# Self-attention of a four-layer transformer block: a lead of 14 query units in place of 22, work by query halves, first operands spread by token halves

## Chip, core and metric

The kernel runs on one core of one Trainium2 chip. The time is the device time of one execution, in microseconds, of which the median of several runs counts. A profile is of one execution.

## What is computed

Two batch entries of 1024 tokens and 256 features pass through four layers. The change is in the self-attention of the third (cut):

```python
x_norm = modulate(_ln(x), shift_a, scale_a)
qkv = x_norm @ W_qkv + b_qkv
q, k, v = jnp.split(qkv, 3, axis=-1)      # 16 heads of 16 features
attn_w = jax.nn.softmax(jnp.einsum('bhqd,bhkd->bhqk', q, k) * scale, axis=-1)
attn_out = jnp.einsum('bhqk,bhkd->bqhd', attn_w, v)
x = x + gate_a[:, None] * (attn_out @ W_proj + b_proj)
```

All is in float32. The layers before (cross-attention, a routed mixture of experts) and behind (cross-attention to a context, two MLPs, windowed attention, attention to the 16 best keys) are not touched.

## The kernel before

There is no planner. Each engine has one program written out by hand, and semaphores tie them. The loop `for b in range(B)` runs over the two batch entries. Within it the self-attention stage works on pairs of heads, eight of them. P is 128 (partitions), T = 8 token tiles, BLK = 512 tokens, TB = 4 tiles in a block, NP = 8 pairs, UNITS = 128.

**Operands.** Queries and keys are kept as a rounded high part and a low part (`dense`: q_hi, q_lo, k_hi, k_lo), so that a score is a product of three terms of 16 rows each, 48 rows. `linear` on TensorE makes the product of one block of tokens, ScalarE (`high_part`, L1434) writes the high part with its bias, VectorE (`low_part`, L2246) the low one. For a pair, `spread(p)` on GpSimd (L2543) copies rows of `dense` to the rows of `qx` and `kx` that the scores read: 12 DMAs of 64 KB a pair, rows 0 to 47 for one head and 64 to 111 for the other. Of `qx` and `kx` there are four places, so pairs 0 to 3 are spread before the loop and pair p + 3 in it. `c_fill` fills four constant rows behind each head's 48.

The `dense` tiles hold eight heads. The other eight are made by `full_step` (L973) on TensorE, from the same block of hT, and copied by ScalarE into `full`, which lies over hT. Once all four pairs have been spread out of `dense`, ScalarE copies `full` over it (L1662), and GpSimd forms the low parts (L2574).

**Units.** A unit is one head and one tile of 128 queries (or keys). `query_scores` (L984) writes 128 queries x 1024 keys with two matmuls; VectorE reduces them to the maximum (`query_maximum`, L2251). After 16 units, a pair, `maxima` (L2256, L2257) splits the maxima in a high and a low part, TensorE transposes them (`turn_maxima`, L991), ScalarE copies them (`maximum_rows`, L1632), and GpSimd sends them by four DMAs (L2553) into rows 48, 49, 112 and 113 of `qx`. So `key_scores` (L999), which writes 128 keys x 512 queries, twice a unit, already subtracts the maximum. ScalarE takes the exponential (`probabilities`, L1640), `weigh_values` (L1011) multiplies with the values, eight matmuls a unit, and `finish` (L1021, L2262) transposes and divides.

**Order.** One loop `for n in range(-LEAD, UNITS)` is written in each engine's program. At step n the key side works on unit n and the query side on unit m = n + LEAD. For the first LEAD steps only query scores are made, for the last LEAD steps only key scores. The query scores take turns in two double banks of PSUM (`take`), the key scores in three banks (`take_key`), so TensorE runs two units ahead of VectorE at most. Steps are in order on each engine: TensorE's wait for the rows of maxima (`mrow_ld`) at the first unit of a pair holds the query scores behind it too.

In the lead TensorE also has four of the eight steps of `full_step`, three small matmuls that spread the gates (L1059), and `keep_busy` (L591): matmuls of a constant tile whose product nobody reads. Ahead of the lead stand `values(1)` (L938), four steps of `full_step` and more `keep_busy`.

The SyncE program loads weights of the layers behind (5.25 MB, L430) while the stage before ends, from 222.8 to 230.3 us.

## Time and profile before

| | us |
|---|---|
| median of 3 runs | 1604.02 (1602.52 to 1604.21) |
| the profiled execution | 1601.8 |
| its span | 1600.0 |
| TensorE matmul busy | 1490.6 (93%) |
| VectorE busy | 1050.8 (66%) |
| ScalarE busy | 769.6 (48%) |
| GpSimd busy | 377.6 (24%) |
| mean granted clock of TensorE | 0.987 |
| self-attention, first query scores to last maximum | 248.3 to 423.4, and again 768 us later |

Busy is the time in which an engine worked; a matmul's end is modelled, so that a busy TensorE can still be one that waits inside. A row in order of time gives the start, the duration, the engine, the line of the kernel, the operation, what it writes and reads, the shapes and how many instructions are merged in it; in brackets how long the engine was idle before and what ended that. Times are from the start of the span. An output of one float32 matmul can be two records.

### The profile page before, as it was taken

How to read it: one execution, taken by the hardware profiler on the slowest of the kernel's cores; microseconds unless marked ns; L12 is line 12 of the kernel's file. 1: busy time of each engine (PE TensorE's matmuls, PEld its weight loads, DVE VectorE, ACT ScalarE, POOL GpSimd, SP SyncE). 2: the span in 40 equal slices, each digit the busy share in tenths (PEclk: the TensorE clock that was granted, in tenths of full speed). 3: DMA queues.
4: the chain of work that ended last, by engine and by line, in shares of the span. 5: the costliest groups of instructions: out<-in, count | busy, mean ns of one | idle time of the engine just before them, and what ended most of it. 6: DMA issues, size and time to landing. Idle time of an engine off the chain costs nothing.

```text
span 1600.0 us, 26614 instructions
## 1 busy us (share of the span) xinstructions
PE 1490.6 (93%) x10593; PEld 937.2 (59%) x10593; DVE 1050.8 (66%) x2960; ACT 769.6 (48%) x1232; POOL 377.6 (24%) x419
## 2 busy tenths in 40 slices
PE   5899999999999999987999999999999999998898
PEld 3457765444355857656765767544445475765676
DVE  2574456999537446899457535599972745579963
ACT  1335421788844533325543543168885363333454
POOL 4420006342125110114133000634210701001330
PEclk9999999999999999999999999999999999999999
DMA  9500037121020000000130001812102000000000
GB/s 339 164 0 1 0 112 106 21 42 22 2 79 1 1 0 3 2 1 1 46 125 1 1 1 61 157 22 36 27 2 79 1 1 1 2 2 1 1 1 27
DMA packets 37663, 59.81 MB, mean 37 GB/s; under 512 B 7347, under 2 KB 27091, under 8 KB 36643
## 3 DMA queue, kind: packets, MB, share of 16 engines
q1 hardware_dynamic: 25239, 34.71, 6.6%
q0 software_dynamic: 9520, 16.04, 6.2%
q10 hardware_dynamic: 2780, 7.36, 1.3%
q8 instruction: 83, 1.36, 0.4%
q14 instruction: 41, 0.34, 0.1%
HBM read 42.22 MB, written 2.10 MB: 28 GB/s over the span
## 4 chain that ended last, share of the span: by engine, by line
PE 66%; DVE 21%; issue 6%; ACT 3%; DMA 1%; POOL 1%; ACTq 0%; DVEq 0%; POOLq 0%
PE ps L999 10%; PE ps L1011 9%; PE ps L463 5%; PE ps L1321 4%; PE ps L984 3%; PE ps L591 3%; PE ps L1112 3%; DVE taken L2384 3%; DVE rs L2062 3%; PE ps L1346 2%; PE ps L1103 2%; DVE taken L2396 2%; DVE mxw L2054 2%; PE ps L1173 2%; PE ps L599 2%
## 5 line engine op out<-in xcount | busy, mean ns | idle before, releaser
L2251 DVE TENSOR_REDUCE mm<-ps 128x1 f32<-128x1024 f32 x256 | 310.5, 1223 | 35.1 <-PE ps L984 31.7
L1640 ACT ACTIVATE pt<-ps 128x512 f32<-128x512 f32 x512 | 276.8, 600 | 61.0 <-PE ps L999 43.6
L2502 POOL TENSOR_TENSOR rstd<-ve,minus_half 128x4 f32<-128x4 f32 x32 | 34.9, 1091 | 695.3 <-DVE ve L1926 695.3
L999 PE MATMUL ps<-qx,kx 64*128 64x512 f32 x512 | 188.5, 445 | 1.0 <-ACT pt L1640 1.0
L984 PE MATMUL ps<-kx,qx 48*128 48x512 f32 x512 | 186.7, 444 | 0.2
L1011 PE MATMUL ps<-pt,v 128*32 128x256 f32 x2048 | 158.7, 390 | 0.0
L999 PEld LDWEIGHTS ps<-qx,kx 64*128 64x128 f32 x512 | 79.0, 184 | 95.9 <-ACT pt L1640 85.9
L591 PE MATMUL ps<-filler 128*128 128x512 f32 x382 | 119.8, 440 | 0.0
L2139 DVE TENSOR_TENSOR rlo<-ring,rhi 128x512 fp32r<-128x512 f32 x48 | 33.2, 691 | 91.9 <-ACT ring L1590 91.9
L1011 PEld LDWEIGHTS ps<-pt,v 128*32 128x32 f32 x2048 | 42.9, 108 | 85.5 <-ACT pt L1640 61.3
L984 PEld LDWEIGHTS ps<-kx,qx 48*128 48x128 f32 x512 | 75.4, 185 | 24.4 <-issue 19.3
L591 PEld LDWEIGHTS ps<-filler 128*128 128x128 f32 x382 | 69.5, 194 | 32.9 <-issue 22.7
L2553 POOL DMA_DIRECT2D qx<-mxT x64 | 33.3, 527 | 209.4 <-ACT mxT L1632 189.3
L2015 DVE TENSOR_TENSOR x<-x,ps 128x512 f32<-128x512 f32 x64 | 41.7, 683 | 50.9 <-PE ps L615 27.5
L1590 ACT ACTIVATE rhi<-ps,mod 128x512 fp32r<-128x512 f32 x48 | 33.1, 690 | 69.1 <-PE ps L783 69.0
L2339 DVE TENSOR_REDUCE mxw<-ps 128x8 f32<-128x1024 f32 x32 | 38.8, 1224 | 37.5 <-PE ps L1173 37.5
L2625 POOL TENSOR_TENSOR prob<-prob,m 128x1024 f32<-128x1024 f32 x16 | 31.0, 1936 | 126.2 <-DVE taken L2384 126.2
L2054 DVE TENSOR_REDUCE mxw<-ps 128x16 f32<-128x1024 f32 x32 | 37.7, 1220 | 34.6 <-PE ps L649 34.6
L1732 ACT ACTIVATE wprobT<-ps 128x1024 f32<-128x1024 f32 x32 | 32.7, 1023 | 56.6 <-PE ps L1199 56.3
L1933 DVE TENSOR_SCALAR xhat<-x,mv,rstd 128x256 f32<-128x256 f32 x128 | 46.3, 425 | 18.9 <-POOL rstd L2502 18.7
L2062 DVE RECIPROCAL rs<-ps 128x512 f32<-128x512 f32 x16 | 53.7, 3355 | 7.3 <-PE ps L686 7.3
L1434 ACT ACTIVATE hT<-ps,mod 128x512 f32<-128x512 f32 x48 | 34.7, 776 | 38.4 <-PE ps L599 38.4
(374 smaller groups left out, 3319.7 us busy)
## 6 DMA issues: line engine op xcount, KB each, us to landing
wm<-in_L_xcond_W_mlp_dram SPq DMA_DIRECT2D x4, 1024.0 KB, 8.6
qx<-q_hi POOLq DMA_DIRECT2D x64, 64.0 KB, 2.5
kx<-k_hi POOLq DMA_DIRECT2D x64, 64.0 KB, 2.5
w3a<-in_L_xcond_w_m_dram SPq DMA_DIRECT2D x2, 2048.0 KB, 7.6
w<-in_L_xcond_e_w_dram SPq DMA_DIRECT2D x6, 512.0 KB, 7.9
w<-in_L_xcond_e_w_dram SPq DMA_DIRECT2D x2, 1536.0 KB, 12.8
s_ada<-in_L_xcond_w_ada_dram ACTq DMA_DIRECT2D x1, 2304.0 KB, 23.3
qx<-q_lo POOLq DMA_DIRECT2D x32, 64.0 KB, 2.4
```

Of the source, the lines that this page charges most:

```text
L463: ins = pe.matmul(ps[:, bank, :], w[:, c, m * P:(m + 1) * P], src[:, c, :], start=c == 0, stop=c == KC - 1)
L591: pe.matmul(ps[:, bank, :], filler[:, 0:P], filler[:, :], start=True, stop=True)
L984: ins = pe.matmul(ps[:, bank + half, :], qx[r, p % 4, t * P:(t + 1) * P], kx[r, p % 4, half * 512:(half + 1) * 512], start=True, stop=True)
L999: pe.matmul(ps[:, bank, :], kx[r, p % 4, kc * P:(kc + 1) * P], qx[r, p % 4, half * 512:(half + 1) * 512], start=True, stop=True).then_inc( ...
L1011: ins = pe.matmul(ps[o:o + 32, 7, q:q + BLK // 2], v2[:, kc, VS * (2 * p + e):VS * (2 * p + e) + 32], pt[:, (2 * kc + e) % 8, half * BLK + ...
L1112: ins = pe.matmul(ps[:, 4 + 2 * k + j, :], w2s[:, wp, m, j * P:(j + 1) * P], gelus[sp][:, m % 4, :], start=m == 0 and (wp, sp) == (0, 0), ...
L1321: ins = pe.matmul(ps[:, 4 + i, :], w3ap[wp][:, c, (NC_HID * i + m) * P:(NC_HID * i + m + 1) * P], src[:, c, :], start=(wp, part, c) == (0, ...
L1640: act.activation(pt[:, u % 8, half * 512:(half + 1) * 512], ps[:, bank, :], ACT.Exp, scale=QK_SCALE).then_inc(st_read, 1)
L2054: ins = dve.tensor_reduce(mxw[:, t, :].rearrange("p (r n) -> p r n", r=4)[:, :, 0:4], ps[:, bank:bank + 4, o:o + D].rearrange("p r (h s) - ...
L2062: link(dve.reciprocal(rs2[:, u % 2, :], ps[:, bank + 1, :]))
L2251: return dve.tensor_reduce(mm[:, p % 2, e, t:t + 1], place(), X, ALU.max).then_inc(ring_read, 1)
L2384: ins = dve.match_replace(taken_by_head(t)[:, h, :], m8[:, t % 2, h, 0:8], scores_by_head(t)[:, h, :], LOWEST)
```

## The change

- LEAD is 14. The first eight units of pair 0 are cut another way: each has both heads, one tile of the first 512 queries, and one half of the keys. After eight units the maxima of the first 512 queries are complete. Their two parts are combined by one more small step.
- Maxima are split, turned, copied and sent after each eight units, the first 512 queries and then the others. A turn has half the rows, and a half is sent by two DMAs of two rows in place of four of one row for the pair.
- Key scores of a unit are now two key tiles against one half of the queries, in place of one key tile against both; `weigh_values` and `probabilities` follow. The wait for rows of maxima stands at every eighth unit.
- Pair 0 is spread by token halves: q_hi, k_hi, q_lo, k_lo of the first 512 tokens ahead of block 1's products, the rest behind. Pair 1 stays on GpSimd; pairs 2 and 3 are issued by ScalarE. The fill comes behind pair 1, and GpSimd waits for its landing.
- `full_step` and `values(1)` move: steps 0 and 1 stand in place of nine fillers, step 2 in place of four, the tiles of values(1) beside units 0 to 3, steps 4 to 7 (some cut in halves) beside units 4 to 9. Their copies on ScalarE are four of 512 columns in place of two of 1024. Fillers stay at units 12 and 13 (two each) and in the first four steps of the key side (one each).

```diff
-N_KEY = 4 * T * NP + NP
+N_KEY = 4 * T * NP + 2 * NP
-LEAD = 22
+LEAD = 14
@@ TensorE
                 linear(2, wqk2, KC, hT[:, 0]).then_inc(full_done, 1)
-                keep_busy(6, 9)
+                full_step(0)
+                full_step(1)
                 ln(2, 1)
-                keep_busy(6, 4)
+                full_step(2)
...
+                    if p == 0 and u < T:
+                        for e in range(2):
+                            r, t, half = slice(64 * e, 64 * e + 3 * HD), u % TB, u // TB
+                            ins = pe.matmul(ps[:, bank + e, :], qx[r, 0, t * P:(t + 1) * P], kx[r, 0, half * 512:(half + 1) * 512],
+                                            start=True, stop=True)
...
-                    kc, e = u // 2, u % 2
+                    half, e, kc = u // T, u % 2, 2 * (u % T // 2) + i
...
-                linear(take() + 1, wqk2, 0, hT[:, 1], (hT_ready, b * 2 * N_HT + 10)).then_inc(ring_ready, 1)
-                linear(take() + 1, wqk2, KC, hT[:, 1]).then_inc(ring_ready, 1)
-                values(1)
-                full_step(0)
-                full_step(1)
-                pe.wait_ge(v_ready, b * NB + NB)
-                full_step(2)
+                linear(take() + 1, wqk2, KC, hT[:, 1], (hT_ready, b * 2 * N_HT + 10)).then_inc(ring_ready, 1)
+                linear(take() + 1, wqk2, 0, hT[:, 1]).then_inc(ring_ready, 1)
                 full_step(3)
                 pe.wait_ge(v2_clear, b + 1)
-                keep_busy(7, 7)
...
-                        if u == 0:
-                            pe.wait_ge(mrow_ld[p % 2], b * N_MROW * NP // 2 + N_MROW * (p // 2 + 1))
+                            pe.wait_ge(gates_ready, b + 1)
+                        if u % T == 0:
+                            pe.wait_ge(mrow_ld[u // T], (b * NP + p + 1) * N_MROW)
                         key_scores(p, u, 0)
-                    if m == 4:
-                        pe.wait_ge(full_ready, b * 2 + 1)
-                    if m >= 4 and n < 4:
-                        keep_busy(4 if m < 2 * T else 7, 3 if n < 0 else 1)
+                    if m == 12:
+                        pe.wait_ge(full_ready, b * 4 + 4)
+                    if m >= 12 and n < 4:
+                        keep_busy(5 if n < 0 else 7, 2 if n < 0 else 1)
                     if m < UNITS:
...
+                        if m == 0:
+                            pe.wait_ge(first_ld, b * N_FIRST + N_SPR)
+                        elif m == TB:
+                            pe.wait_ge(first_ld, b * N_FIRST + N_FIRST)
...
-                    if m < 4:
-                        full_step(m + 4)
+                    if m < TB:
+                        values(1, (m,))
+                    elif m == 4:
+                        pe.wait_ge(full_ready, b * 4 + 1)
+                        full_step(4, slice(0, 2 * P))
+                    elif m == 5:
+                        full_step(5, slice(0, 2 * P))
+                        full_step(4, slice(2 * P, BLK))
+                    elif m == 6:
+                        full_step(5, slice(2 * P, BLK))
                     elif m == 7:
-                        pe.wait_ge(full_ready, b * 2 + 2)
+                        pe.wait_ge(v_ready, b * NB + NB)
+                        full_step(6)
+                    elif m == 8:
+                        full_step(7, slice(0, 2 * P))
+                    elif m == 9:
+                        full_step(7, slice(2 * P, BLK))
+                    elif m == 11:
+                        pe.wait_ge(full_ready, b * 4 + 3)
...
-                    if at_m == 1 and 1 <= q <= NP:
-                        turn_maxima(q - 1)
+                    if at_m == 9 and q < NP:
+                        turn_maxima(q, 0)
+                    elif at_m == 1 and 1 <= q <= NP:
+                        turn_maxima(q - 1, 1)
@@ ScalarE
+                act.wait_ge(ring_ready, u0 + 1)
+                high_part(1, 1, 1)
+                act.wait_ge(ring_ready, u0 + 2)
+                high_part(0, 1, 3)
+                act.wait_ge(full_done, b * 6 + 4)
+                full_part(0, 0, 7)
+                act.wait_ge(hi_ready, b * 6 + 4)
+                act.wait_ge(ring_read, u0 + 2)
+                spread(2)
+                act.wait_ge(full_done, b * 6 + 5)
+                full_part(0, 1, 7)
+                act.wait_ge(v_done, b * NB + NB)
+                spread(3)
+                act.wait_ge(full_done, b * 6 + 6)
+                full_part(1, 0, 6)
+                full_part(1, 1, 5)
                 act.wait_ge(gates_spread, b + 1)
...
+                act.wait_ge(early_ld, b * 2 * N_SPR + 2 * N_SPR)
                 for qk in range(2):
                     act.activation(dense[2 * qk][:, :], full[qk], ACT.Copy).then_inc(hi_ready, 1)
@@ VectorE
                 statistics(b, 2, 1)
+                low_part(0, 0, 0).then_inc(lo_ready, 1)
                 normalise(b, 2, 1)
...
                         query_maximum(q, at_m)
-                        if at_m == 2 * T - 1:
-                            maxima(q)
+                        if m == TB - 1:
+                            add_v2(1)
+                        if at_m % T == T - 1:
+                            maxima(q, at_m // T)
@@ GpSimd
+                pool.wait_ge(hi_ready, b * 6 + 1)
+                part(0, 0, 0, low, first_ld)
+                ln(2, (1,))
+                pool.wait_ge(hi_ready, b * 6 + 2)
+                part(1, 0, 0, low, first_ld)
...
-                for p in range(3):
-                    spread(p)
+                pool.wait_ge(lo_ready, b * 4 + 1)
+                part(0, 1, 0, low, first_ld)
+                pool.wait_ge(lo_ready, b * 4 + 2)
+                part(1, 1, 0, low, first_ld)
+                pool.wait_ge(first_ld, b * N_FIRST + N_SPR)
+                part(1, 0, 0, high, first_ld)
...
+                part(0, 1, 0, high, spread_ld[0])
+                spread(1)
                 pool.wait_ge(v_done, b * NB + NB)
...
-                spread(3)
+                pool.wait_ge(fill_ld, b * 64 + 64)
                 for p in range(NP):
-                    maximum_rows(p)
+                    maximum_rows(p, 0)
...
                     if p >= 1 and p + 3 < NP:
-                        spread(p + 3)
+                        spread(p + 3, (0,))
+                    maximum_rows(p, 1)
+                    if p >= 1 and p + 3 < NP:
+                        spread(p + 3, (1,))
```

## Rows read from the trace of the kernel before

**Rows 1.** TensorE in order of time, lead (start, us, engine, line, what, count)

```profile
239.69 3.62 PE L938 MATMUL ps<-wv,hT 128*128 128x256 f32 x16
...
248.29 0.73 PE L984 MATMUL ps<-kx,qx 48*128 48x512 f32 x2
248.95 1.12 PE L973 MATMUL ps<-hT,wqk 128*128 128x512 f32 x2
...
256.50 0.97 PE L591 MATMUL ps<-filler 128*128 128x512 f32 x3
...
283.26 0.40 PE L999 MATMUL ps<-qx,kx 64*128 64x512 f32 x1
...
1016.31 0.73 PE L984 MATMUL ps<-kx,qx 48*128 48x512 f32 x2
```

**Rows 2.** VectorE in order of time, lead; idle time in brackets

```profile
243.34 1.29 DVE L2179 TENSOR_TENSOR v<-ps,vb 128x512 f32<-128x512 f32 x2 [1.91 <-PE ps L938]
...
258.16 1.23 DVE L2251 TENSOR_REDUCE mm<-ps 128x1 f32<-128x1024 f32 x1 [0.33 <-PE ps L984]
```

**Rows 3.** GpSimd in order of time, its DMA issues

```profile
232.26 1.01 POOL L2502 TENSOR_TENSOR rstd<-ve,minus_half 128x4 f32<-128x4 f32 x1 [29.93 <-DVE ve L1926]
...
239.49 2.04 POOL L2543 DMA_DIRECT2D qx<-q_hi  x4 [5.82 <-ACT q_hi L1434]
...
263.52 1.12 POOL L2543 DMA_DIRECT2D kx<-k_lo  x2
278.27 2.07 POOL L2553 DMA_DIRECT2D qx<-mxT  x4 [13.63 <-ACT mxT L1632]
```

**Rows 4.** DMA issues of the whole program: count, KB each, median us to landing

```profile
qx<-q_hi POOLq DMA_DIRECT2D x64, 64.0 KB, 2.5
...
qx<-mxT POOLq DMA_DIRECT2D x64, 4.0 KB, 1.6
```

**Rows 5.** ScalarE in order of time, lead

```profile
239.89 0.69 ACT L1434 ACTIVATE k_hi<-ps,colT 128x512 fp32r<-128x512 f32 x1 [1.03 <-PE ps L463]
...
273.05 1.06 ACT L1662 ACTIVATE q_hi<-hT 128x1024 fp32r<-128x1024 f32 x1 [10.35 <-DMA kx<-k_lo]
...
277.42 0.27 ACT L1632 ACTIVATE mxT<-ps 32x128 fp32r<-32x128 f32 x1 [2.36 <-PE ps L991]
```

**Rows 6.** Busy time by stretch: length, five engines, PEclk, DMA share, GB/s

```profile
224.00:238.00 14.00, 12.94 (x48) 7.15 (x47) 8.83 (x21) 2.82 (x4) 1.41 (x3) 1.00 0.95 317
240.00:258.00 18.00, 18.00 (x57) 9.41 (x55) 8.16 (x8) 2.81 (x3) 17.89 (x39) 1.00 0.72 132
258.00:272.00 14.00, 14.00 (x48) 7.32 (x48) 10.83 (x9) 0.87 (x2) 6.64 (x14) 1.00 1.13 131
```

**Rows 7.** VectorE in order of time, one pair of the steady part

```profile
318.06 4.81 DVE L2251 TENSOR_REDUCE mm<-ps 128x1 f32<-128x1024 f32 x4
...
323.69 12.25 DVE L2251 TENSOR_REDUCE mm<-ps 128x1 f32<-128x1024 f32 x10
336.38 2.45 DVE L2251 TENSOR_REDUCE mm<-ps 128x1 f32<-128x1024 f32 x2 [0.44 <-PE ps L984]
...
339.18 4.82 DVE L2251 TENSOR_REDUCE mm<-ps 128x1 f32<-128x1024 f32 x4
```

**Rows 8.** TensorE in order of time, first units of the tail

```profile
422.59 0.73 PE L999 MATMUL ps<-qx,kx 64*128 64x512 f32 x2
...
423.82 0.73 PE L999 MATMUL ps<-qx,kx 64*128 64x512 f32 x2
```

**Rows 9.** Issues of loads by ScalarE and SyncE in order of time

```profile
6.49 0.48 ACTq L1445 DMA_DIRECT2D s_mod<-in_L_xcond_W_mod_dram  x1
...
225.24 1.71 SPq L430 DMA_DIRECT2D wqkv<-in_L_xcond_w_qkv_dram  x1
```

**Rows 10.** Busy time by stretch, around a fall of TensorE's clock

```profile
833.90:840.70 6.80, 3.76 (x63) 2.33 (x66) 4.15 (x4) 1.28 (x2) 6.72 (x2) 1.00 0.04 10
840.70:844.11 3.41, 3.41 (x34) 1.81 (x32) 2.36 (x2) 1.28 (x1) 3.41 (x2) 0.50 0.02 5
```

More of the change, by code:

```diff
@@ L2521, in _, with part @@
                 ln(1)
[L2522 to L2524 removed]
+                ln(2, (0,))
+                def part(qk, part, p, cols, done):
+                    wide = (qx, kx)[qk]
+                    for e in range(2):
+                        r = 32 * (p % 4) + HD * e
+                        for i in range(3):
+                            if ((0, 1, 0), (0, 0, 1))[qk][i] == part:
+                                pool.dma_start(wide[64 * e + HD * i:64 * e + HD * (i + 1), p % 4, cols], dense[2 * qk + part][r:r + HD, cols]).then_inc(done, 16)
```

218 lines of the change are left out of this document (118 added, 100 removed).

## Prediction, made before the changed kernel was built or timed

> **What bounds the kernel now.** I read the stage from its front to its back: TensorE's order of time, VectorE's, GpSimd's and ScalarE's, the DMA share by stretch, then the steady part and the tail. The self-attention stage runs once a batch, the second time 768.02 us after the first with the same steps [rows 1], so each term below is worked out once and doubled.
>
> TensorE first. The first unit's query scores start at 248.29 and the first key score at 283.26 [rows 1]: the lead of 22 units takes 34.97 us, 1.59 us a unit. The three rows between show what fills it: a unit's two score matmuls (0.66 us from start to start), then one step of the key and query products (1.12 busy) for four units, then three filler matmuls (0.97 busy) for the rest. VectorE needs 1.23 us for a maximum and is idle for 0.33 before it [rows 2], as before most of them there. So in the lead the filler sets the pace, 1.56 us a unit, and VectorE has a fifth to spare.
>
> What lets the lead begin at 248.29? GpSimd issues the first spread from 239.49 on, a DMA every 0.48 us, 36 spreads of three pairs, the fill, 12 spreads more up to 264.5 [rows 3]; a 64 KB spread lands 2.5 us after its issue [rows 4]. Twelve from 239.49 land at about 247.9. TensorE uses the time for values(1) [rows 1], four product steps and fillers.
>
> What lets the keys begin at 283.26? Not the maxima's rows alone. ScalarE copies the second products into the dense tiles at 273.05, after 10.35 us of waiting for the last spread to land [rows 5], copies the turned maxima at 277.42, and GpSimd issues their four rows at 278.27 [rows 3]; those land in 1.6 us [rows 4]. The DMA engines are at 0.72 of their time between 240 and 258, while GpSimd issues, and at 1.13 in the next 14 us, where the fill and the last 12 spreads drain [rows 6]. This backlog is the resource to watch.
>
> In the steady part a pair of 16 units takes 339.18 - 318.06 = 21.12 us [rows 7], 1.32 a unit: 16 maxima at 1.22, 0.35 for splitting them, 0.82 for finish (323.69 - 322.87), 0.44 idle. VectorE sets it; TensorE's own work is 1.23 a unit. A unit without query scores starts 1.23 after the one before, too [rows 8].
>
> **The parts and their costs.**
>
> Start of the lead. q_hi of the first 512 tokens goes out at about 229, k_hi after the rstd of 232.26 to 233.27 [rows 3], both low parts by 237.8. They share the engines with the weight loads (share 0.95 from 224 to 238 [rows 6]), so I let the last land at 240.2. TensorE's own work decides then: the second product of block 1 ends at about 239.9 (its copy, k_hi at 239.89 [rows 5]), full_step(3) adds 0.9. First unit at 240.8, 7.5 us earlier.
>
> Pace. In units 0 to 3 a tile of values(1) stands beside the scores: 3.62 us for four [rows 1], 0.9 each, with the scores' 0.66 some 1.6 us a unit. Then half steps of 0.56 us lie beside the 1.23 of VectorE, which is the bound with add_v2(1) (1.3 by the same line's row [rows 2]) and the first split (0.5, three small steps for two). Sum: 4 x 1.6 = 6.4, add_v2 and unit 3's rest 1.7, units 4 to 11 8 x 1.23 = 9.8, split 0.5, the scores of unit 13 and fillers 1.2. TensorE comes to unit 0's key score at 240.8 + 19.6 = 260.4. The removed fillers cost 0.33 a unit before; nothing is late in their place but the maximum itself.
>
> ScalarE. It now issues 24 spreads. No row shows such a DMA from it; a load of 1.5 MB took it 0.48 us to issue, SyncE needed 1.71 for one of half the size [rows 9]. Ends: 0 and 1.71; I take 0.45, nearest to its own row. spread(2) is issued from 241.5 to 246.9. full_part(0,1) waits for unit 6's product, 251.3; spread(3) then goes from 252.0 to 257.4, two copies of 0.69 [rows 5] to 258.8, the gates' 768 elements, by the same row 1.0, to 259.8. Queued behind the issues are these copies, for which TensorE waits at units 11 and 12.
>
> DMA. The work before was 0.72 x 18 = 13.0 us for 36 spreads, 0.36 each, and 14 us for the fill with 12 spreads. Of 27, about 2 now fall before 240. If two queues bring the engines to their limit at once and no further, the spreads end at 240.3 + 25 = 265; if they add up without loss, the last lands 2.5 after its issue, at 259.9. From the landing to the key score: two dense copies 2.0 and the turned maxima 0.3 [rows 5], GpSimd's step 0.6 (277.69 to 278.27) and two DMAs in place of four 1.0 [rows 3], landing 1.6 [rows 4], sum 5.5. So the first key score lies between 265.4 and 270.5. Both rows are equally near: the share of 1.13 speaks for the late end, and that the fill no longer stands ahead of spread(3) in one queue for the early one. I take 268.5: 14.8 us earlier than 283.26.
>
> The Trainium skill (DMA: Bandwidth & Descriptors, Issuing engines are not separate DMA queues) has it that issuing from several engines saves only the sequencer's issue time, since all run on the same 16 DMA engines. It speaks against this part of the change; by it alone the late end holds, 270.5, and the sum would be 4 us smaller over both batches.
>
> Units moved. Eight units lose their place in the lead (their gain is within the 14.8) and get query scores in the main loop: 8 x (1.32 - 1.23) = 0.7 lost. The 22 units of the tail become 14, the 106 of both become 114.
>
> Maxima in halves. A pair splits twice. The gap of a split is 339.18 - 338.83 = 0.35 [rows 7], on VectorE, which is the bound: 8 x 0.35 = 2.8 us. Below: 0, if it goes into the 0.44 idle of each pair. Above: 0.35 + 0.44, if each brings such a stall. I take 2.7. TensorE's eight more transposes and ScalarE's eight copies (0.27 [rows 5]) lie beside it: TensorE has 21.12 - 16 x 1.23 = 1.4 us a pair beside its units; without that cover they would cost up to 0.3 each, 2.4, and 2.2. The rows of maxima are asked for five units after their turn, as before: 6.6 us for a chain of 0.3 + 0.6 + 1.0 + 1.6 = 3.5. GpSimd's spread of the next pair, cut into 6 and 6, puts 2.9 us in that chain at most, and just fits.
>
> Clock. TensorE waits from 260.4 to 268.5 with nothing to do. Before, it had a stretch busy for 3.76 of 6.80 us and then 3.41 at a granted clock of 0.50, which is 1.2 GHz [rows 10]. Here it has nothing at all for 8 us, so I let the level last 5. In that time units of 1.23 become 2.46 where 1.32 are asked: 2 us lost. Ends: 0 (no wait) and 3.
>
> Nothing: the order of key blocks and query halves in key scores and values (same shapes and counts), the new bank numbers, the fill's wait (it lands before the rows), the other form of the first eight units (the same 1024 elements a maximum).
>
> Sum a batch: -14.8 + 0.7 + 2.7 + 2.0 = -9.4 us. Both: -18.8. The profiled execution, 1601.8 us around a span of 1600.0, would be 1583.0; it is 2.2 under the median of 1604.02, so the median comes to 1585. No stage behind this one waits for a load that the shift would uncover (the weights they read were issued before the lead, in the 0.95 of 224 to 238 [rows 6]).
>
> **The rivals.**
>
> The queues add up. Then the first key score is at 265.4, 17.9 early, TensorE idles 5 us, and the clock costs 1: -17.9 + 3.4 + 1.0 = -13.5 a batch, 1577. For: 0.72 with one queue, 0.36 us of engine a spread. Against: 1.13 in the drain. Chance 0.25.
>
> Stalls at each half. Twice the turns, each a place where TensorE, ScalarE and GpSimd follow one another; at 0.79 for each split and 3 for the clock the batch gains 14.8 - 0.7 - 6.3 - 3 = 4.8, time 1594. Against it, the slack of 6.6 over 3.5. Chance 0.12.
>
> The lead is not shortened: DMA holds the keys. With a drain as slow as that of 258 to 272 for all that is left and the clock's 3 us, the keys start at 276 or 277 and the gain is 0 to 1, 1602 to 1604. This is also the case in which the change doesn't do what it says. Chance 0.07.
>
> Slower. ScalarE's issues take as long as SyncE's longest, 1.71 [rows 9], as its queue fills while the engines are behind. 24 of them put 41 us on ScalarE, from 241.5 to 282.5; behind them are 3.1 of copies and gates, then 5.5: key score at 291, 8 late, and +8 + 3.4 + 2 = 13 a batch, 1631. It decides from 278 on (there the 5.4 of the other terms are eaten), so from (278 - 5.5 - 3.1 - 241.5) / 24 = 1.16 us an issue. Against it: 0.48 for 24 times the bytes. Chance 0.05.
>
> **How the numbers follow.** My forecast has the remaining 0.51, at 1585, with its own range of 1578 to 1592. A measurement of this kernel tells 0.2%, 3.2 us, from no change. Faster by more: forecast 0.51, adding queues 0.25, stalls 0.11, together 0.87; same 0.06; slower 0.07. The range of 1572 to 1599 takes in the two larger rivals with their unknown costs and leaves out the last two.
>
> **What would show it.** First query scores near 240.8, reductions without idle time from unit 4 to 11; ScalarE's spread issues near 0.45; the dense copies' wait for DMA ending between 260 and 265; the first key score at 265 to 271 behind a TensorE wait for the rows of maxima; 0.50 of clock behind it; pairs of 21.4 to 21.5. Wrong would be: a key score before 264 or after 273, issues over 1 us, pairs over 21.9.

## The result and the profile after

The changed kernel is slower: 1610.12 us median of 20 runs (1600.26 to 1620.27) against 1604.63 of 20 runs of the kernel before, ratio 1.0038 with a 95% interval of 1.0022 to 1.0053. 1585 was forecast, and the range of 1572 to 1599 does not hold it. The profiled execution took 1609.57 us, its span is 1607.8, the mean granted clock of TensorE 0.965 (0.987 before).

Everything up to the stage is 1.27 us later in this profile: GpSimd's rstd stands at 233.53 (232.26 before [rows 3]). Profiles differ in this by themselves: the first copy into kpair of the whole program, far ahead of the change, stands at 51.74 before, at 52.68 here and between 50.96 and 54.75 in the experiments. Times from the first query score on are therefore the better ones to compare. TensorE in order of time, the lead-in and the first key scores:

```profile
242.46 0.50 PE L996 MATMUL ps<-kx,qx 48*128 48x512 f32 x2 [0.27 <-issue]
...
257.35 0.73 PE L1002 MATMUL ps<-kx,qx 48*128 48x512 f32 x2 [0.24 <-DVE mm L2318]
260.67 1.01 PE L1094 MATMUL ps<-row_hl,row_of 128*128 128x256 f32 x3 [2.59 <-ACT hT L1471]
...
264.76 1.22 PE L1002 MATMUL ps<-kx,qx 48*128 48x512 f32 x2
277.21 0.76 PE L1017 MATMUL ps<-qx,kx 64*128 64x512 f32 x1 [11.23 <-DMA qx<-mxT]
...
289.21 1.08 PE L1031 MATMUL ps<-pt,v 128*32 128x256 f32 x8
```

The first unit is 5.8 us earlier than the 248.29 of [rows 1], 7.1 without the later front. The first key score is only 6.05 earlier than 283.26. Between them are two waits: 2.59 us behind unit 11, for ScalarE's copies into hT, and 11.23 us for the maxima's rows. From 262.46 on the same two score matmuls take 1.22 us in place of 0.73 (the row of 264.76 is the second such): half clock. The stretches of the same kernel (length, then busy time of TensorE, its weight loads, VectorE, ScalarE, GpSimd, then the granted clock, DMA share, GB/s):

```profile
240.00:258.00 18.00, 17.39 (x61) 8.30 (x59) 15.60 (x18) 2.40 (x4) 13.47 (x28) 1.00 0.93 138
258.50:271.00 12.50, 5.31 (x11) 2.64 (x11) 3.50 (x3) 2.14 (x4) 0.00 (x0) 0.50 1.02 106
277.20:286.40 9.20, 9.19 (x20) 4.39 (x20) 4.01 (x5) 3.85 (x7) 3.48 (x2) 0.50 0.00 0
286.40:296.10 9.70, 9.70 (x54) 4.20 (x53) 6.03 (x5) 5.04 (x10) 1.11 (x2) 0.50 0.02 3
296.10:300.00 3.90, 3.90 (x40) 1.37 (x36) 3.46 (x5) 3.32 (x7) 0.00 (x0) 1.00 0.00 0
```

The granted clock is 0.50, 1.2 GHz, from 258.5 to 296.1, 37.5 us, and in the second batch for 34.1 us from 1033.4. Before, it never fell in this stage. In the first batch the fall stands at 258.5, when the last product had ended 0.5 us before (257.35 + 0.73); most of the 2.59 us without work comes behind it. TensorE is busy without a gap for the last 19 us of it. The DMA share is 0.93 where it was 0.72 [rows 6], so the queues do overlap, but it stays at 1.02 for 12.5 us more.

ScalarE in order of time:

```profile
243.00 2.95 ACTq L1696 DMA_DIRECT2D qx<-q_hi  x4
...
258.63 1.25 ACTq L1696 DMA_DIRECT2D kx<-k_lo  x2
259.93 1.26 ACT L1471 ACTIVATE hT<-ps,colT 128x512 f32<-128x512 f32 x2 [6.92 <-issue]
...
271.96 1.06 ACT L1723 ACTIVATE q_hi<-hT 128x1024 fp32r<-128x1024 f32 x1 [9.38 <-DMA kx<-k_lo]
272.93 1.04 ACT L1723 ACTIVATE k_hi<-hT 128x1024 fp32r<-128x1024 f32 x1
273.87 0.25 ACT L1669 ACTIVATE mxT<-ps 16x128 fp32r<-16x128 f32 x1
```

The 24 issues end at 259.88, and the copies on which unit 11 waits start behind them (their 6.92 of idle is issue time). The dense copy at 271.96 is 1.1 us earlier than the 273.05 of [rows 5], behind a wait as long (9.38 and 10.35). GpSimd: the first operands' low parts land at 242.9, and the maxima's rows leave at 274.84.

```profile
242.95 1.93 POOL L2601 DMA_DIRECT2D kx<-k_hi  x4 [4.16 <-DMA kx<-k_lo]
...
254.36 1.10 POOL L2654 DMA_DIRECT2D qx<-in_c_fill_dram  x2
...
274.84 1.13 POOL L2620 DMA_DIRECT2D qx<-mxT  x2 [18.42 <-ACT mxT L1669]
```

The steady part answers to [rows 7]: a pair takes 340.99 - 319.71 = 21.28 us on VectorE, against 21.12.

```profile
319.71 4.81 DVE L2318 TENSOR_REDUCE mm<-ps 128x1 f32<-128x1024 f32 x4
...
340.99 1.22 DVE L2318 TENSOR_REDUCE mm<-ps 128x1 f32<-128x1024 f32 x1
```

The stage ends where the next one forms kpair on VectorE, at 455.39 before and 458.29 after:

```profile
458.29 0.48 DVE L2001 TENSOR_TENSOR kpair<-kT,parity 128x128 f32<-128x128 f32 x2
```

So from the first key score to kpair it took 172.13 us and now takes 181.08. What was won ahead of the keys (6.05) is lost behind them (8.95), and the batch ends 2.90 us later; the second adds 4.1.

Of the runs below one of e5, two of e7 and one of e15 were disturbed; the medians count them, the ratios do not.

### The profile page after: what moved, and what is told of

The parts are those of the page before. It is cut to its first block, busy times and chain, and to the rows that moved or that the text cites. A ratio compares the mean times of both kernels' runs of the same rounds, so it can differ in the third digit from the quotient of the medians.

```text
span 1607.8 us, 26526 instructions
## 1 busy us (share of the span) xinstructions
PE 1465.0 (91%) x10481; PEld 921.6 (57%) x10481; DVE 1053.9 (66%) x2994; ACT 772.3 (48%) x1252; POOL 368.7 (23%) x395
## 4 chain that ended last, share of the span: by engine, by line
PE 66%; DVE 22%; ACT 3%; DMA 3%; issue 3%; SPq 1%; POOL 1%; ACTq 1%; DVEq 0%; POOLq 0%
PE ps L1017 10%; PE ps L1031 9%; PE ps L471 6%; PE ps L1358 4%; PE ps L881 3%; PE ps L1149 3%; DVE taken L2455 3%; DVE rs L2125 3%; DVE taken L2467 3%; PE ps L859 2%; PE ps L1383 2%; PE ps L1140 2%; DVE mxw L2117 2%; PE ps L1210 2%; DMA kx<-k_lo 2%
## 5 line engine op out<-in xcount | busy, mean ns | idle before, releaser
L2318 DVE TENSOR_REDUCE mm<-ps 128x1 f32<-128x1024 f32 x240 | 289.3, 1221 | 56.2 <-PE ps L1002 53.7
L1017 PE MATMUL ps<-qx,kx 64*128 64x512 f32 x512 | 196.4, 463 | 22.8 <-DMA qx<-mxT 21.9
L1031 PE MATMUL ps<-pt,v 128*32 128x256 f32 x2048 | 162.0, 397 | 0.0
L1017 PEld LDWEIGHTS ps<-qx,kx 64*128 64x128 f32 x512 | 83.6, 192 | 114.7 <-ACT pt L1677 73.8
L599 PE MATMUL ps<-filler 128*128 128x512 f32 x242 | 80.1, 463 | 0.0
L2078 DVE TENSOR_TENSOR x<-x,ps 128x512 f32<-128x512 f32 x64 | 41.7, 682 | 51.1 <-PE ps L623 27.6
L599 PEld LDWEIGHTS ps<-filler 128*128 128x128 f32 x242 | 48.1, 208 | 18.3 <-issue 10.9
```

The source lines that it names most:

```text
L599: pe.matmul(ps[:, bank, :], filler[:, 0:P], filler[:, :], start=True, stop=True)
L1017: pe.matmul(ps[:, bank, :], kx[r, p % 4, kc * P:(kc + 1) * P], qx[r, p % 4, half * 512:(half + 1) * 512], start=True, stop=True).then_inc( ...
L1031: ins = pe.matmul(ps[o:o + 32, 7, half * 2 * P:(half + 1) * 2 * P], v2[:, kc, VS * (2 * p + e):VS * (2 * p + e) + 32], weights[:, :, part, ...
L2318: return dve.tensor_reduce(mm[:, p % 2, e, t:t + 1], place().rearrange("p a q -> p (a q)"), X, ALU.max).then_inc(ring_read, 1)
```

## The experiments

Theory A: TensorE's waits in the lead-in let the clock fall, and that costs the most. Theory B: the spreads and the fill keep the DMA engines busy, so that the dense copies, and the maxima's copy queued behind them on ScalarE, come late whatever the lead is. Rivals: a lead of 14 is too short by itself; ScalarE as issuer is at fault; the halves cost more than 0.35 us each. The recorded expectations use letters of their own: the A of e1 is this A, its B is the moved units and halves, and what they call C is this B. The table has, for every run, the median, the ratio to the kernel before in the same session with its interval, and of the profile's first batch the first query score, the time from it to the first key score, kpair (the end of the stage), and the stretch at 0.50 in the stage.

| kernel | median us | ratio | first query | to key | kpair | at 0.50 |
|---|---|---|---|---|---|---|
| before | 1604.63 | | 248.29 | 34.97 | 455.39 | none |
| after | 1610.12 | 1.0038 [1.0022, 1.0053] | 242.46 | 34.75 | 458.29 | 37.5 |
| e1 | 1595.34 | 0.9950 [0.9932, 0.9967] | 242.82 | 35.14 | 451.56 | none |
| e2b | 1619.11 | 1.0090 [1.0075, 1.0104] | 243.46 | 43.85 | 468.00 | 44.4 |
| e3 | 1624.40 | 1.0124 [1.0091, 1.0157] | 242.60 | 39.09 | 462.32 | 41.0 |
| e4 | 1597.07 | 0.9959 [0.9942, 0.9976] | 242.10 | 27.02 | 450.70 | 30.7 |
| e5 | 1610.26 | 1.0034 [1.0014, 1.0053] | 244.41 | 36.70 | 461.47 | 34.1 |
| e6 | 1588.45 | 0.9909 [0.9877, 0.9941] | 242.02 | 26.01 | 446.92 | 13.7 |
| e7 | 1619.13 | 1.0051 [1.0021, 1.0080] | 248.05 | 34.97 | 455.14 | none |
| e8 | 1601.82 | 0.9979 [0.9968, 0.9991] | 241.38 | 27.61 | 450.75 | 20.5 |
| e9 | 1601.49 | 0.9982 [0.9972, 0.9991] | 242.86 | 30.89 | 455.22 | 23.9 |
| e10 | 1620.30 | 1.0103 [1.0080, 1.0126] | 241.38 | 34.55 | 462.79 | 37.5 |
| e11 | 1609.54 | 1.0036 [1.0024, 1.0048] | 248.02 | 30.79 | 458.93 | 41.0 |
| e12 | 1596.17 | 0.9935 [0.9913, 0.9956] | 243.01 | 29.70 | 451.90 | 13.7 |
| e13 | 1603.73 | 1.0013 [0.9987, 1.0038] | 240.70 | 39.07 | 453.38 | 10.2 |
| e14 | 1597.45 | 0.9950 [0.9931, 0.9970] | 242.28 | 28.36 | 447.17 | 3.4, 3.4 |
| e15 | 1592.73 | 0.9913 [0.9892, 0.9935] | 241.66 | 30.34 | 456.06 | 23.9 (tail) |
| e16 | 1590.05 | 0.9916 [0.9902, 0.9930] | 242.85 | 30.03 | 447.95 | none |

In the second batch the stretches at 0.50 are 6.8 us in e6, 6.8 and 27.3 in e7, 3.4 and 17.1 in e12, 17.1 in e14, and none in e1, e15 and e16; elsewhere they are within 3.5 us of the first's.

### The clock: e1, e13, e10, e11

**e1** fills both waits of the changed kernel with products that nobody reads.

```diff
                         if n == 0:
-                            pe.wait_ge(fill_ld, b * 64 + 64)
                             pe.wait_ge(gates_ready, b + 1)
+                            keep_busy(7, 56)
+                            pe.wait_ge(fill_ld, b * 64 + 64)
...
                     elif m == 11:
+                        pe.wait_ge(full_ready, b * 4 + 2)
+                        keep_busy(7, 12)
                         pe.wait_ge(full_ready, b * 4 + 3)
```

> The changed kernel with 12 filler matmuls before TensorE's wait of unit 11 and 56 before its wait for the rows of maxima at the first key score; nothing else. Theory A (the wait lets TensorE's granted clock fall to 0.50, and it stays there for some 19 us after the keys begin): the first key score stays where it is, 34 to 35 us after the first query score, but the granted clock is 1.00 there, and each batch ends about 7 us earlier: 1594 to 1598. Theory B (the eight units that moved into the main loop and the second split of the maxima cost the time, the clock next to nothing): 1608 to 1611, as the change itself.

Two stretches of e1 and the first key score:

```profile
258.50:271.00 12.50, 12.50 (x51) 8.89 (x51) 4.41 (x4) 2.14 (x4) 0.00 (x0) 1.00 1.04 114
271.00:278.00 7.00, 6.87 (x32) 5.39 (x30) 0.00 (x0) 3.45 (x4) 2.41 (x3) 1.00 0.02 2
```

```profile
277.96 0.46 PE L1017 MATMUL ps<-qx,kx 64*128 64x512 f32 x1
```

The clock holds, the key start and the DMA share stay as they were (1.04), and 1610 becomes 1595. From the first key score to kpair it is now 173.60, in both batches: the low clock cost 181.08 - 173.60 = 7.5 us (7.0 in the second batch), and the moved units and the halves together 173.60 - 172.13 = 1.5. That the low clock costs this, and that work in the waits holds the clock up, is shown by this; what remains is B.

**e13** is e1 with the 56 fillers at the keys alone.

> The changed kernel with 56 fillers at the wait for the first maxima rows alone, none at the wait of unit 11. If the idle ahead of unit 11 is what lets the clock fall, it falls at about 258 as in the changed kernel and stays low until values matmuls run, for the fillers have not lifted it elsewhere: 1607 to 1612. If the 11 us ahead of the first key score is what holds it down, the clock falls for a few microseconds at most or not at all: 1595 to 1600, as with both waits filled.

```profile
256.00:259.50 3.50, 0.54 (x4) 0.26 (x3) 1.79 (x2) 1.06 (x2) 0.00 (x0) 0.99 0.94 98
259.50:269.70 10.20, 10.20 (x24) 6.44 (x24) 2.45 (x2) 1.08 (x3) 0.00 (x0) 0.50 0.93 103
269.70:279.70 10.00, 10.00 (x45) 8.05 (x43) 0.00 (x0) 3.44 (x4) 5.91 (x4) 1.00 0.02 3
```

The fall comes at the end of the wait of unit 11 (2.96 us here), as without any fillers; those at the keys then bring the clock back before the keys, 10.2 us later in place of 37.5. The fillers are slower meanwhile and hold the keys until 279.77. In time it lies between the two forecasts (1603.73, unclear against before).

The wait of unit 11 is not needed for a fall, though. In e3, described below, TensorE has no such wait:

```profile
257.52 0.73 PE L1002 MATMUL ps<-kx,qx 48*128 48x512 f32 x2 [0.27 <-DVE mm L2306]
258.18 0.71 PE L1094 MATMUL ps<-row_hl,row_of 128*128 128x256 f32 x3
```

```profile
256.00:258.50 2.50, 2.23 (x9) 1.08 (x9) 2.50 (x3) 1.27 (x2) 2.50 (x7) 1.00 0.80 146
258.60:262.00 3.40, 3.40 (x9) 1.45 (x7) 2.20 (x2) 0.87 (x2) 3.40 (x8) 0.50 1.03 190
```

The clock falls at the same 258.5 with 0.27 us of idle time ahead of it. In e14 it falls at 258.1 with 0.26 us, while TensorE is working on the 12 fillers that it shares with e1, and is back 3.4 us later; in e1, e15 and e16 TensorE has the same steps up to there and no fall. So the fillers in both waits kept the clock up in e1, but what starts a fall in this lead, and why one execution has it and another not, is not shown.

**e10** asks whether dense matmuls in the key steps lift the clock sooner: four fillers in place of one.

```diff
-                        keep_busy(5 if n < 0 else 7, 2 if n < 0 else 1)
+                        keep_busy(5 if n < 0 else 7, 2 if n < 0 else 4)
```

> The changed kernel with four filler matmuls in place of one in each of the first four steps of the key side; the wait before them is untouched. Theory A1 (the granted clock rises again only when matmuls over all 128 rows come; scores have 48 and 64 rows): the stretch at 0.50 ends about 7 us after the first key score, near 285 in place of 296, and the time falls by 4 to 9 us. Theory A2 (any busy TensorE lifts it in its own time): the stretch ends as late, and the fillers cost 12 x 0.43 = 5 us a batch, 1616 to 1621.

```profile
276.00:293.00 17.00, 17.00 (x41) 9.50 (x41) 6.15 (x7) 5.94 (x12) 4.35 (x4) 0.50 0.00 0
293.00:298.00 5.00, 5.00 (x34) 1.81 (x36) 3.19 (x4) 2.82 (x6) 0.19 (x1) 0.50 0.04 5
```

They don't: 17.00 of 17.00 us busy at 0.50, and the clock rises at 298.0, some 5 us behind the first values matmul (293.05). In the changed kernel these two are 289.21 and 296.1, in e4 281.11 and 289.2, in e12 282.74 and 289.0. The fillers only add their own time.

**e11** is the kernel before without the fillers of units 4 to 21, a change to the old lead alone.

```diff
-                        keep_busy(4 if m < 2 * T else 7, 3 if n < 0 else 1)
+                        keep_busy(4 if m < 2 * T else 7, 0 if n < 0 else 1)
```

> The kernel before without its fillers in units 4 to 21 of the lead. Theory C: VectorE's 1.23 us a unit brings TensorE to the first key score 5 to 6 us earlier, at 277.5 to 279, where it waits for the rows of maxima behind the dense copies at 273. Theory A: TensorE then does 0.66 us of work over 48 rows in each 1.23 and the clock falls in the lead, which costs more than the 5 us: 1605 to 1625. Without theory A: 1592 to 1598.

```profile
257.70:278.80 21.10, 18.08 (x34) 8.24 (x35) 19.11 (x19) 4.32 (x6) 10.04 (x20) 0.50 0.76 89
278.80:290.80 12.00, 11.99 (x28) 5.86 (x28) 6.34 (x6) 5.93 (x11) 3.46 (x2) 0.50 0.00 1
```

The keys start 4.2 us sooner behind the first query score, and the kernel is 0.36% slower: 41.0 us at half clock. So the fillers that paced the old lead also held its clock, at a price of 4.2 us.

### The lead's length: e2b

LEAD back to 22, one more wait for the gates at unit 16, two fillers in each further unit.

```diff
-LEAD = 14
+LEAD = 22
...
+                    if m == 2 * T:
+                        pe.wait_ge(gates_ready, b + 1)
...
-                        keep_busy(5 if n < 0 else 7, 2 if n < 0 else 1)
+                        keep_busy(5 if m < 2 * T else 7, 2 if n < 0 else 1)
```

> The changed kernel with LEAD at 22 again (its fillers in bank 7 from unit 16 on, behind a wait for the gates). Theory C (the keys begin when the DMA engines are done): first key score within 2 us of the changed kernel's 277.2, though eight more units stand ahead of it. Theory A (the clock is what the wait costs): the eight units fill most of the wait, the granted clock behind it is 1.00 or back at 1.00 within 10 us; 1594 to 1600. If the short lead itself were worth its 8 units, this kernel would be slower than the changed one with fillers (1595), by more than 5 us; theory A says within 3 of it.

The clock falls at 262.2 and the longer lead then runs at half speed, 2.30 us a unit (two scores and two fillers, 1.22 each), for 44.4 us; all forecasts (1594 to 1600, keys at 277) missed. The price is paid on whatever stands behind the fall, and with the clock low e2b can't say what a lead of 22 is worth here. Against a lead of 14 being too short stands e1: with the clock held it is 0.5% faster than the kernel before, which has 22.

### Who issues, and what the DMA engines carry: e3, e5, e4, e6, e7

**e3** gives the spreads of pairs 2 and 3 back to GpSimd, in front of and behind the fill; **e5** gives them to SyncE.

```diff
                 spread(1)
+                spread(2)
                 pool.wait_ge(v_done, b * NB + NB)
...
+                spread(3)
                 pool.wait_ge(fill_ld, b * 64 + 64)
```

> The changed kernel with pairs 2 and 3 spread by GpSimd again, in the order spread 1, spread 2, fill, spread 3; ScalarE issues none. Theory C (the DMA engines are at their limit, and it doesn't matter who issues): the dense copies' wait for the last spread ends within 2 us of the 272.0 of the changed kernel, the time within 3 us of it, though ScalarE's copies for units 11 and 12 are no longer late. Theory D (ScalarE's issues of 0.62 us and the copies queued behind them set the end): the wait ends more than 4 us earlier.

> The changed kernel with pairs 2 and 3 issued by SyncE in place of ScalarE. Theory C (DMA engines at their limit): TensorE no longer waits at unit 11 and ScalarE's copies are early, but the dense copies still start within 2 us of 272; 1604 to 1612, with the clock falling later. Theory D (ScalarE's queue sets the end): the dense copies start more than 4 us earlier, 1590 to 1600.

```profile
240.00:258.00 18.00, 17.02 (x60) 8.23 (x58) 15.46 (x18) 3.42 (x6) 14.90 (x32) 1.00 0.53 95
```

That is e3: with one queue the share is 0.53 where two gave 0.93, the dense copy stands at 276.45 (271.96) and the key 4.3 us later from the first query (39.09 against 34.75). Neither forecast held. GpSimd's last spread is issued at 268.2, where ScalarE's was at 259.9. So the second queue is worth about 4 us of the key start here, and one issuer alone was a limit. The median is 14 us over the changed kernel's; its six runs go from 1615.87 to 1631.40, and what stands behind that beyond 4.3 us a batch is open. SyncE in ScalarE's place frees the copies (they run at 258.90 behind TensorE's product, not behind issues), but the dense copy comes at 275.85 (31.4 us behind the first query score, 29.5 in the changed kernel) and the time is that of the changed kernel: the issuer's name is not the fault. It also takes away the wait of unit 11, and the clock falls at 264.3 all the same, 1.0 us into the 17.84 us that TensorE waits for the keys. The Trainium skill (DMA: Bandwidth & Descriptors, Issuing engines are not separate DMA queues) says that issuing on several engines saves only the sequencer's time; these runs agree, and show that this time was some 4 us of the lead.

**e4** makes the key scores read 50 rows in place of 64 and fills two rows of kx by two DMAs in place of four DMAs of 256 KB. It leaves out 14 rows that are constant and add nothing to the scores.

```diff
-KA = 4 * HD
+KA = 3 * HD + 2
...
-                for i, wide in enumerate((qx, kx)):
-                    for e in range(2):
-                        pool.dma_start(wide[64 * e + 3 * HD:64 * e + KA, :, :], g["c_fill"][i]).then_inc(fill_ld, 16)
+                for e in range(2):
+                    pool.dma_start(kx[64 * e + 3 * HD:64 * e + KA, :, :], g["c_fill"][1][0:2]).then_inc(fill_ld, 16)
```

> The changed kernel with 50 rows in place of 64 in the key scores, so that the fill is two rows of kx a head (two DMAs of 32 KB in place of four of 256 KB); the 14 rows of zeros left out change no score. Theory C (DMA engines at their limit): the work of the fill, 8 to 10 us, is gone, the dense copies start at 261 to 264 in place of 272, the first key score at 267 to 269, the wait of TensorE shrinks to 3 us; with less time at 0.50 of clock 1580 to 1592. Theory D: the fill lies beside other work and costs nothing: 1606 to 1611.

The DMA issues of the changed kernel (count, KB each, median us to landing), and below them the same of e4:

```profile
kx<-k_hi ACTq DMA_DIRECT2D x16, 64.0 KB, 8.1
...
kx<-in_c_fill_dram POOLq DMA_DIRECT2D x4, 256.0 KB, 13.4
...
kx<-k_lo ACTq DMA_DIRECT2D x8, 64.0 KB, 8.4
```

```profile
kx<-k_hi ACTq DMA_DIRECT2D x16, 64.0 KB, 3.8
...
kx<-k_lo ACTq DMA_DIRECT2D x8, 64.0 KB, 4.1
```

Without the fill ScalarE's spreads of the keys land in 3.8 to 4.1 us in place of 8.1 to 8.4 (those of q_hi in 4.1 in place of 4.3):

```profile
263.83 1.06 ACT L1723 ACTIVATE q_hi<-hT 128x1024 fp32r<-128x1024 f32 x1
```

```profile
269.12 0.76 PE L1017 MATMUL ps<-qx,kx 50*128 50x512 f32 x1 [2.03 <-DMA qx<-mxT]
```

The dense copy stands at 263.83, straight behind ScalarE's other copies and no longer behind a DMA, and the first key score at 269.12, where 268.5 had been predicted. Theory B is shown for the fill: its traffic was 8.1 us of the key start, 7.7 counted from the first query score. The clock still falls for 30.7 us, and 1597 is what is left, above the 1580 to 1592 expected.

**e6** joins e4, SyncE as issuer and 24 fillers ahead of the keys.

> All three: pairs 2 and 3 issued by SyncE, 50 rows in the key scores with a fill of two rows, 24 fillers in the wait before the first key score. By the sums: the spreads land at 259 to 261, the dense copies start there, the first key score 24 to 26 us after the first query score in place of 35; 173.6 us from the first key score to the end of the stage as in the run with fillers; 1572 to 1580. If theory C is wrong about the fill and theory D about the issues, 1590 to 1595.

1588.45, above the 1572 to 1580 expected, and in its profile the earliest kpair (446.92). The clock falls at 270.6 all the same, behind 1.7 us without work ahead of the first key score.

**e7** is e4's edit in the kernel before.

> The kernel before with 50 rows in the key scores and the fill of two rows; nothing else. Its lead of 22 units is paced by fillers, which bring it to 283.3 whenever the spreads land: the dense copies start at 265 to 267 in place of 273, the first key score stays within 1 us, 1601 to 1606, the same. If the DMA engines held its keys, they would begin 5 us or more earlier and the time would be 1590 to 1595.

The dense copy comes 7.8 us earlier (265.28), the key not at all: 34.97 us from the first query, as before. The old lead was paced by its units and not by the DMA engines. That corrects the reading of [rows 5, 6]: its ScalarE waited 10.35 us for a spread, and nothing waited for ScalarE. But 1601 to 1606 was expected and 1619.13 measured: in the second batch the clock falls in the tail, where only key scores and values run:

```profile
1200.00:1209.20 9.20, 8.72 (x72) 3.23 (x70) 0.49 (x2) 8.34 (x17) 0.00 (x0) 1.00 0.01 2
1209.20:1236.50 27.30, 27.30 (x152) 9.68 (x144) 0.75 (x3) 11.47 (x22) 0.00 (x0) 0.50 0.00 1
```

e15 shows the same in one of its two batches; with 64 rows the longest fall there was 3.4 us (e10). But e4 and e6 have 50 rows as well and no fall in the tail in either batch, and two runs of e7 (1604.55 and 1606.68) are as fast as the kernel before, with mean granted clocks of 0.986 and 0.984 where the profiled run has 0.974. So the cause of these falls is open; that it has to do with the rows is argued from two profiles.

### The order of the chain: e8, e9, e12, e14, e16

**e8**, with all 64 rows and the whole fill, takes the maxima out from behind the dense copies: ScalarE sends the first half before it waits for the spreads, copies the second operands behind unit 4, GpSimd's low parts go behind the second half's rows, and the fill ahead of pair 1; 12 and 8 fillers.

```diff
-                act.wait_ge(early_ld, b * 2 * N_SPR + 2 * N_SPR)
-                for qk in range(2):
-                    act.activation(dense[2 * qk][:, :], full[qk], ACT.Copy).then_inc(hi_ready, 1)
...
                     if n >= 0:
                         probabilities(p, u)
+                    if n == 4:
+                        second_operands()
```

> The changed kernel, and in it: ScalarE sends the first maxima on before it waits for the spreads and copies the second operands (the copies go behind unit 4's probabilities, GpSimd's low parts behind the second rows of maxima), GpSimd issues the fill ahead of pair 1, and 12 and 8 fillers stand in TensorE's waits. Theory E (the keys are held by the order on ScalarE, which ties them to the landing of pairs 2 and 3, not by the DMA engines as such): the first key score comes 24 to 27 us after the first query score in place of 35, and the time is 1572 to 1582. Theory C in its plain form (the engines' 27 us of work stand ahead of the keys whatever the order): 33 us or more, 1593 to 1598.

> The same with pairs 2 and 3 issued by SyncE, and fillers only before the first key score. Theory E: the gates and the first maxima no longer queue behind the issues, the first key score comes 20 to 23 us after the first query score, 1565 to 1575. If the clock falls in the lead all the same (TensorE does 0.66 us of scores in 1.23 at units 10 to 13), up to 10 us more.

In e8 the key comes 27.6 us after the first query in place of 34.8, but the two DMAs of the rows, issued from 262.11 on, take 6.2 us to land, and in the 4.09 us of idle that this leaves the clock falls at 268.0. e9, with SyncE for the spreads, is no better (1565 to 1575 was expected). **e12** has 28 fillers in place of 8, **e14** has 20 and SyncE sends the first rows:

> The changed kernel in the order of e8 (maxima of the first half sent before ScalarE waits for the spreads, dense copies of the second operands behind unit 4), with 28 fillers in place of 8 while TensorE waits for the first maxima rows, so that its idle of 4.1 us there is filled. Theory A (the clock falls because TensorE idles ahead of the first key scores): granted clock 1.00 through the stage, first key score 27.6 to 28.8 us after the first query score as in e8, about 7 us more saved in each batch than there: 1582 to 1590. Rival (the fall in e8 comes from the queueing of values behind the late dense copies, or from the key scores themselves): the clock falls again near 268 and the time stays at 1598 to 1604.

> e12 with 20 fillers, and with the first maxima's two rows sent by SyncE in place of GpSimd, whose queue holds the fill and the spread of pair 1. If they were late because of what stands ahead of them on that queue (6.9 us from issue to landing in e8, 1.6 us in the kernel before), they land about 2 to 3 us after their issue here, the first key score comes about 25 us after the first query score, and the time is 1575 to 1585. If the DMA engines are simply full, the landing stays at 5 to 7 us and the time is that of e12 within 3 us.

The landing of the first rows in e8 and in e12, both issued by GpSimd (the last lines of the answers on the tile mxT, from 255 to 272):

```profile
DMA to landing us min/median/max: 6.2/6.2/6.2
```

```profile
DMA to landing us min/median/max: 8.3/8.4/8.5
```

In e14 SyncE issues them from 263.9 to 265.5. Its semaphore also counts ScalarE's spreads, so that the profile gives no landing for them, but the packets tell. q1 is SyncE's queue, q0 GpSimd's, q10 ScalarE's; from 263.9 to 268.8, and from 268.8 to 269.8:

```profile
q10 hardware_dynamic: 239, 0.50, 77.7%
q0 software_dynamic: 166, 0.31, 41.6%
```

```profile
q10 hardware_dynamic: 30, 0.03, 16.0%
q1 hardware_dynamic: 20, 0.01, 4.9%
```

In the first 4.9 us no packet of the rows is moved, though nothing else stands in SyncE's queue; all 20 come in the next microsecond, when GpSimd's traffic is over and ScalarE's ends. So the rows wait for the traffic on the engines whichever queue they are in, and GpSimd's own queue was not the fault. That is the second of e14's two forecasts (5 to 7 us, the time of e12 within 3 us: 1597.45 and 1596.17). With nothing else under way two such rows land in 1.7 us (the changed kernel's median). In e12 the clock fell again, at 275.4, behind 1.69 us without work:

```profile
272.71 0.46 PE L1017 MATMUL ps<-qx,kx 64*128 64x512 f32 x1 [1.69 <-DMA qx<-mxT]
```

**e16** is e14 with 36 fillers.

> e14 with 36 fillers in place of 20 while TensorE waits for the first maxima rows. In e12 TensorE sat 1.7 us ahead of the first key score and the clock fell at 275.4; in e14 it sat 1.6 us in the stretch and fell at 282.0. If these last gaps are what still lets it fall, 36 fillers keep it at 1.00 and the time is 1585 to 1592; if the fall comes from the late dense copies or from the order itself, the time stays at 1595 to 1600.

```profile
257.00:264.00 7.00, 6.75 (x26) 4.01 (x26) 3.68 (x4) 3.33 (x6) 0.15 (x1) 1.00 1.14 137
264.00:273.00 9.00, 9.00 (x39) 6.93 (x39) 1.72 (x2) 0.23 (x1) 0.00 (x0) 1.00 0.65 87
273.00:300.00 27.00, 26.02 (x210) 10.80 (x214) 23.35 (x25) 23.04 (x43) 9.88 (x12) 1.00 0.10 16
```

No stretch of the stage is at 0.50 in either batch, and its six runs lie close together (1588.33 to 1592.86): 1590.05, faster than both kernels. The order by itself costs little: from first key to kpair 175.07 against e1's 173.60. So 16 more fillers ahead of the keys took away the falls behind them (at 282.0 in e14's first batch, at 1032.9 in its second). The fall of 3.4 us at 258.1 stands ahead of these fillers and is not explained by them.

**e15** takes both causes away in the simpler way, e1's two waits filled (12 and 36) and e4's small fill.

> The changed kernel with both causes taken away at once: the fill cut to the 50 rows that the key scores then read (as in e4, where the first key score stood at 269.1, what the prediction had), and fillers in both waits of the lead-in, 12 and 36 (as in e1). Theory A (what was predicted was lost to the clock and to the late dense copies, nothing else): granted clock 1.00 through the stage, first key score 27 to 29 us after the first query score, first kpair copy about 443 to 446, and 1582 to 1590, which is the predicted 1585. Rival (the steady phase of the shorter lead is slower for a reason of its own, or matmuls over 50 rows let the clock fall later): 1593 to 1600 with the key start as early.

1592.73, just above the 1582 to 1590 expected. The second batch, at full clock, goes from first query to kpair in 203.99 us where the kernel before took 207.10. In the first the clock falls in the tail, at 428.8, for 23.9 us. Its fillers run to the 272.00 of the first key score; e4's stood at 269.12. So 1585 was reached neither here nor elsewhere in a median; e6 and e16 stand nearest.

## Why the prediction was wrong

**Start of the lead: right.** 240.8 forecast, 242.46 measured, 241.2 without the later front. The low parts landed at 242.9 and not at 240.2, but the first units did not need that.

**Pace: the first part right.** Units 0 to 3 start 1.49 us apart (1.6 forecast). TensorE came to the key's wait at 266.0 and not 260.4, for the wait behind unit 11 and the half clock. This by itself moved no key, as the rows came at 277.

**ScalarE: a size off, and its consequence missed.** 0.67 us an issue (243.00 to 251.56 and 252.32 to 259.88 for 24) against 0.45. The prediction named the copies queued behind the issues and the units 11 and 12 that wait for them, and put them on no path. They leave TensorE 2.59 us without work at unit 11, the place where the clock falls (258.5) and where e1's fillers keep it up.

**DMA: the failing step for the key start.** "The spreads end at 240.3 + 25 = 265" was its late end. By the shares they took 0.93 x 18 + 1.02 x 12.5 = 29.5 us from 240 on, and the last half microsecond that the two rows leave out (258.0 to 258.5) adds to it; the dense copy came at 271.96. The sum took 0.36 us of engine time a spread from a stretch with a single queue and counted the 14 us at a share of 1.13 as 14 and not 15.8; with two queues and the fill at once the same work took more, and e4 shows that the fill is what made it late. From the copy to the key 5.5 was forecast and 277.21 - 271.96 = 5.25 measured. First key score: 6.05 early, not 14.8. The rival that let the DMA hold the keys had this right (276 or 277), at a chance of 0.07.

**Clock: the second failing step.** "I let the level last 5" and 2.0 us. It lasted 37.5 and 34.1, and cost 7.5 and 7.0. The prediction counted the units that run slow as if the clock came back soon after the keys; it came back only 6.9 us behind the first values matmuls. It also placed the fall in the wait for the keys; it came ahead of that wait, at 258.5. The price was taken from [rows 10], a fall of 3.41 us in another kind of work.

**Moved units and halves: overpriced.** 3.4 forecast, 173.60 - 172.13 = 1.5 measured in e1. A pair grew by 0.16 us for one split more, not 0.35.

**The sum.** First batch: -6.05 + 1.5 + 7.5 = +2.9, which is 458.29 - 455.39. It took both failing steps to turn the sign: with the clock priced at 2.0 it would be -2.6, with the keys 14.8 early -5.8, and e1 and e4, which take away one each, are both faster than the kernel before. In the second the first query is 1.5 us earlier than before and kpair 7.0 later, and the span is 7.8 longer. Of the rivals none held the result: stalls at the halves did not occur, and ScalarE's issues stayed under the 1.16 us from which the slower case was to decide. It went slower by two mechanisms of the forecast itself: the drain of the DMA engines, past its late end, and the clock, whose upper end of 3 us was too low.

## What to carry to other kernels

Find every place where a reordering thins out TensorE's work, a wait of 2.6 us included, and price it by all the work that then runs at half clock (37.5 us), not by the wait; filling the waits with products that nobody reads was worth 15 us in e1, but no single wait was shown to be what starts a fall. Where a critical start hangs on a copy behind a DMA, test the traffic, the number of issuing queues and the order of the waits one by one: each was worth 4 to 8 us here. Moving a small urgent DMA to an empty queue was worth nothing while the engines were loaded (e14). A long wait in the old trace does not name a bound: e7 took 7.8 us off one and nothing moved.

## What was not expected of the hardware

The clock fell with only 0.27 us (e3) and 0.26 us (e14) of idle time ahead of it. It stayed at 0.50 through 17.00 of 17.00 us of scores and fillers in e10 and rose only some 5 to 8 us behind the first values matmuls, yet fillers alone brought it back in e13 in the 5.3 us from 264.36 to 269.7, and in e14 at 261.5. Which property of the work decides is open.

The Trainium skill (TensorE: Matmul & The Clock Gate, HAM oscillation — how this bites in real kernels) has it that a wait for a DMA between matmuls lets the engine fall back to the low clock. The traces of e5 and e8 agree: the clock falls at 264.3 and at 268.0, while TensorE waits 17.84 and 4.09 us for the rows. That it also falls behind 0.27 us, and then lasts through 19 us of unbroken work, is seen in the rows above and not in that section.

Four DMAs of 256 KB to 16 rows each doubled the landing of 64 KB spreads of k_hi on another queue (8.1 against 3.8 us). Two DMAs of two rows each took 6.2 and 8.4 us to land on GpSimd's loaded queue (e8, e12), and on SyncE's empty one no packet of them moved for 4.9 us (e14), until the other queues' traffic was nearly over.
